# Expert up products taken in fp32 as they lie, instead of in three products of fp32r halves

## What is computed

```python
def moe_ff(x, gate_w, w1, w2, w3):
    scores = xf @ gate_w
    topk_scores, topk_idx = jax.lax.top_k(scores, TOPK)
    topk_probs = jax.nn.softmax(topk_scores, axis=-1)
    weight = jnp.sum(jax.nn.one_hot(topk_idx, EXPERTS, dtype=xf.dtype) * topk_probs[..., None], axis=1)
    h = jax.nn.silu(jnp.einsum('td,edh->eth', xf, w1)) * jnp.einsum('td,edh->eth', xf, w2)
    out_e = jnp.einsum('eth,ehd->etd', h, w3)
    out = jnp.einsum('etd,te->td', out_e, weight)
```

## Time and profile before

| | |
|---|---|
| time, median of 3 runs | 2132.61 us (2127.89 to 2138.53) |
| the profiled execution | 2133.48 us, its span on the core 2131.9 us |
| granted TensorE clock, mean | 0.852 |
| TensorE busy over the span | 1599.4 us (75%) in 19079 matmul instructions |
| VectorE busy | 1275.6 us (60%) |
| ScalarE busy | 1043.0 us (49%) |
| GpSimd busy | 347.0 us (16%) |
| up products (L1410) | 384 matmul instructions into `e_ps_a`, 384 into `e_ps_b` |
| down products (L1425) | 256 matmul instructions |

### The profile page before, as it was taken

One profiled execution on the slowest core, in us unless ns is written; L12 is line 12 of the kernel. 1 busy time (PEld: TensorE's weight loads), 2 busy tenths in 40 slices (PEclk: granted clock), 3 DMA queues, 4 the chain that ended last, 5 costly groups with the idle time before them and its releaser, 6 DMA issues. The chain is left out here.

```text
span 2131.9 us, 53638 instructions
## 1 busy us (share of the span) xinstructions
PE 1599.4 (75%) x19079; PEld 991.3 (46%) x19079; DVE 1275.6 (60%) x3054; ACT 1043.0 (49%) x1996; POOL 347.0 (16%) x677
## 2 busy tenths in 40 slices
PE   6544477777539999975349988798889788989647
PEld 3222244444326666643125555455555455556423
DVE  6932776676256766743206666565667565667636
ACT  4422166566323233214236666565667466667233
POOL 4433254454320000002200000000000000000023
PEclk8866599899659999987658999898989798889869
DMA  2157222222451211217898999898999899999521
GB/s 69 45 167 225 58 64 55 55 64 47 117 179 45 94 70 54 102 36 210 244 294 294 345 354 345 306 359 292 370 337 360 302 337 352 343 350 331 175 66 59
DMA packets 189941, 424.95 MB, mean 199 GB/s; under 512 B 37296, under 2 KB 85328, under 8 KB 180272
## 3 DMA queue, kind: packets, MB, share of 16 engines
q1 hardware_dynamic: 165856, 241.52, 36.9%
q10 hardware_dynamic: 13104, 150.80, 17.3%
q0 software_dynamic: 10720, 29.11, 5.3%
HBM read 218.07 MB, written 203.03 MB: 198 GB/s over the span
## 5 line engine op out<-in xcount | busy, mean ns | idle before, releaser
L2133 DVE CUSTOM_DVE_ANT_0 r_shifted<-r_ps_ac,r_shifted 128x512 f32<-128x512 f32 x512 | 352.1, 688 | 336.0 <-PE r_ps_ac L2010 319.4
L2099 ACT ACTIVATE r_probs<-r_ps_keys 128x512 f32<-128x512 f32 x512 | 309.5, 605 | 296.8 <-PE r_ps_keys L2017 262.3
L2078 ACT ACTIVATE r_wide<-r_ps_wide 128x512 f32<-128x512 f32 (+1 forms) x576 | 329.2, 590 | 72.2 <-PE r_ps_wide L2001 71.0
L2017 PE MATMUL r_ps_keys<-r_ident,r_shifted 128*128 128x128 f32 x2048 | 337.2, 291 | 3.4 <-issue 1.4
L2017 PEld LDWEIGHTS r_ps_keys<-r_ident,r_shifted 128*128 128x128 f32 x2048 | 277.0, 151 | 62.9 <-issue 20.2
L2001 PE MATMUL r_ps_wide<-r_r,r_qv 48*32 48x64 bf16 (+12 forms) x6144 | 240.9, 259 | 50.8 <-issue 34.1
L2010 PE MATMUL r_ps_ac<-r_k,r_qu 128*128 128x512 bf16 x512 | 214.1, 419 | 68.6 <-DMA r_v<-v 31.7
L2141 DVE TENSOR_SCALAR r_shifted<-r_shifted,r_mx 128x512 f32<-128x512 f32 x512 | 249.2, 487 | 18.3
L915 ACT ACTIVATE c_probs<-c_ps_keys 128x512 f32<-128x512 f32 (+1 forms) x384 | 174.8, 531 | 152.2 <-PE c_ps_keys L841 152.0
L2001 PEld LDWEIGHTS r_ps_wide<-r_r,r_qv 48*32 48x32 bf16 x6144 | 103.8, 96 | 151.4 <-issue 150.0
L2028 PE MATMUL r_ps_out<-r_probs,r_v 128*9 128x128 f32 x4096 | 155.7, 290 | 23.7 <-issue 23.0
(11 more groups left out here) (215 smaller groups left out, 2106.2 us busy)
## 6 DMA issues: line engine op xcount, KB each, us to landing
skew<-r_wide ACTq DMA_DIRECT2D x64, 2224.0 KB, 11.8
r_shifted<-skew SPq DMA_DIRECT2D x64, 2048.0 KB, 17.2
e_weight_all<-weights SPq DMA_DIRECT2D x8, 2048.0 KB, 7.5
c_qk<-qk_stacks POOLq DMA_DIRECT2D x64, 192.0 KB, 3.7
stack<-d_part SPq DMA_DIRECT2D x96, 128.0 KB, 2.6
qk_stacks<-b_part SPq DMA_DIRECT2D x48, 128.0 KB, 3.4
qk_stacks<-b_part POOLq DMA_DIRECT2D x48, 128.0 KB, 3.7
stack<-d_part POOLq DMA_DIRECT2D x48, 128.0 KB, 3.8
```

The costliest lines, as they stand in the source:

```text
L2017: last = pe.transpose(ps_keys[u % 2][:, j * P:(j + 1) * P], shifted[:, s, u, j * P:(j + 1) * P], ident[:, :])
L2078: act.activation(wide[:, s, c, lo:hi], ps_wide[bk % BANKS][:, 0:hi - lo], ACT.Copy).then_inc(wide_sb, 1)
L2099: act.activation(probs[:, h % 2, :, b * P:(b + 1) * P], ps_keys[u % 2][:, :].rearrange("p (j i) -> p j i", j=NT), ACT.Exp, scale=SCALE).th ...
L2133: dve.tensor_tensor_reduce(out=shifted[:, s, u, :], in0=ps_ac[u % 2][:, :], in1=shifted[:, s, u, :], scale=1.0, scalar=LOWEST, op0=ALU.add ...
```

## The change

w1, w2 and `hT` are handed to TensorE as they are, in fp32. The half tiles, the casts and subtractions on DVE and POOL, and their semaphores go. `up` issues one matmul for each k instead of three. In the loop, TensorE waits for `hT` itself (`hT_sb`) ahead of the first product of a new block. At the start, the up products of expert 0 wait for their own weights alone and are issued ahead of `turn_weights(0)`, where they stood behind it.

```diff
             def up(w, ps, e, s, ready):
                 for k in range(KH):
-                    for i, (a, b) in enumerate(HALVES):
-                        last = pe.matmul(ps[:, k, :], w[a][:, e, k * P:(k + 1) * P], hT_halves[b][:, s, :],
-                                         start=(i == 0), stop=(i == 2))
+                    last = pe.matmul(ps[:, k, :], w[:, e, k * P:(k + 1) * P], hT[:, s, :], start=True, stop=True)
                 last.then_inc(ready, 1)
...
                         if e + 2 == NE:
-                            pe.wait_ge(hT_low, n + 2)
+                            pe.wait_ge(hT_sb, n + 2)
                         ups(n + 1, 1 - s, e + 2 - NE)
...
             pe.wait_ge(consts, n_const)
             route(0, 0, 16)
+            pe.wait_ge(w_loaded[0], 16)
+            up(w1, ps_a, 0, 0, a_ps)
+            pe.wait_ge(w_loaded[1], 16)
+            up(w2, ps_b, 0, 0, b_ps)
             turn_weights(0)
-            pe.wait_ge(hT_low, 1)
-            pe.wait_ge(w_low, 1)
-            up(w1_halves, ps_a, 0, 0, a_ps)
-            pe.wait_ge(w_low, 2)
-            up(w2_halves, ps_b, 0, 0, b_ps)
             ups(0, 0, 1)
             pe.wait_ge(w_loaded[2], 16)
             steps(step, pe)
...
                     if e == 0 and ahead:
                         best(n + 1)
-                        high_tokens(n + 1, 1 - s)
...
             best(0)
-            high_tokens(0, 0)
             weights(0)
             take_rows(0)
-            for i, (w, halves) in enumerate(((w1, w1_halves), (w2, w2_halves))):
-                dve.wait_ge(w_loaded[i], 16)
-                high(halves[0][:, :, :], w[:, :, :], w_high)
-                dve.wait_ge(w_high, i + 1)
-                dve.tensor_tensor(halves[1][:, :, :], w[:, :, :], halves[0][:, :, :],
-                                  ALU.subtract).then_inc(w_low, 1)
             for e in range(2):
                 product(e, e, 0, 1)
```

More of the change, by code:

```diff
@@ L1221, in phase_experts @@
         w3 = sb("w3", [P, NE, HID])
-        w1_halves = [sb(f"w1_half{i}", [P, NE, HID], F32R) for i in range(2)]
-        w2_halves = [sb(f"w2_half{i}", [P, NE, HID], F32R) for i in range(2)]
         gate = sb("gate", [P, NE])
@@ L1230, in phase_experts @@
         hT = sb("hT", [P, 2, L])
-        hT_halves = [sb(f"hT_half{i}", [P, 2, L], F32R) for i in range(2)]
         scores = sb("scores", [P, NT, NE])
@@ L1278, in phase_experts @@
         gu_sb = sem("gu_sb")
[L1279 to L1282, removed]
         w_loaded = [sem(f"w{i}_loaded") for i in (1, 2, 3)]
@@ L1359, in _ @@
         def _(pool):
[L1360 to L1363, removed]
             def step(it, s, first, ahead):
@@ L1367, in step @@
                 for e in range(NE):
-                    if e == 0 and ahead:
-                        low_tokens(n + 1, 1 - s)
                     if e == 3 and not first:
@@ L1373, in _ @@
             norm.constants(pool)
-            low_tokens(0, 0)
             steps(step, pool)
@@ L1379, in _ @@
         def _(pe):
-            HALVES = ((0, 0), (0, 1), (1, 0))
             def route(n, s, load_count):
@@ L1416, in ups @@
                 pe.wait_ge(silu_sb, m + 1)
-                up(w1_halves, ps_a, e, s, a_ps)
+                up(w1, ps_a, e, s, a_ps)
                 pe.wait_ge(gu_sb, m + 1)
-                up(w2_halves, ps_b, e, s, b_ps)
+                up(w2, ps_b, e, s, b_ps)
             def down(m, s, e):
@@ L1537, in take_rows @@
                 dve.tensor_copy(weight_rows[:, :], ps_s[0:NE, 0:L]).then_inc(rows_sb, 1)
[L1539 to L1544, removed]
             def product(m, e, s, loads):
```

## The result

| | before | changed |
|---|---|---|
| time, median | 2130.25 us (2122.72 to 2138.53, 4 runs) | 2155.26 us (2149.89 to 2166.61, 4 runs) |
| ratio | | 1.0142, 95% interval 1.0101 to 1.0183 |
| the profiled execution | 2133.48 us, span 2131.9 | 2153.25 us, span 2151.8 |

Two further sets of runs of the changed kernel gave 1.0109 (1.0068 to 1.0150) and 1.0116 (1.0075 to 1.0157). So the direction was right and the size too large by some 15 us (+40.4 forecast). Ratios are of fast executions alone: the profile of e3 is of a slow one (1201.10 us), and of e10's six executions one of 6671.60 us is left out of its ratio.

A forecast was written before the change was run, and what follows sets the result against it. It took TensorE's instruction issue to bound the experts' loop. 2133.5 us profiled + 38.7 (loop) + 1.7 (start) = 2173.9; that execution being 0.9 above the median, the forecast was 2173.0 us, range 2165 to 2182.

The forecast's parts named there:

- The loop: Experts' loop: each of 61 rounds grows from 4.51 to 5.15 us on TensorE, +38.7 us (36.6 to 40.9).
- Passes against rows: Up products: passes alone give 0.93 us more a round; the trace's durations give 0.635, which the forecast took.
- The start: Experts' start: first product 9.7 us earlier, but the spread load lands later; first down product +1.7 us (-1.6 to +5).
- (1): Rival: the start keeps its 9.7 us because the spread load lands in time; 2161.6 us, chance 0.03.
- (2): Rival: passes alone count, so the loop's up products grow by a third, 56.9 us; 2191 us, chance 0.03.
- (3): Rival: each fp32 up instruction streams like a half product, 0.233 us, gaining 0.93 a round; 2077 us, chance 0.02.
- (4): Rival: the clock doesn't hold 1.00 in the loop with more fp32; about 2215 us, chance 0.04.
- The later phases shifted alone: Phases behind the experts: they would start later but keep their lengths, so they add nothing to the sum.

The follow-up runs named there:

- e3: The kernel before without the phase of relative attention, the merge reading the first attention's sums instead: 1185.92 us.
- e10: The changed kernel with 160 semaphore increments on TensorE at the start of the relative attention: 2189.47 us, ratio 1.0274.
- e4: The changed kernel without the phase of relative attention, the merge reading the first attention's sums instead: 1228.34 us.
- e16: The kernel before with TensorE semaphore increments: 40 at the experts' start, 40 at their end, 80 at the relative attention's start: 2116.69 us, ratio 0.9937.
- e13: The kernel before with 80 semaphore increments at the end of TensorE's experts and 80 at the relative attention's start: 2122.31 us, ratio 0.9974.
- e14: The changed kernel with 80 semaphore increments at the end of TensorE's experts and 80 at the relative attention's start: 2182.30 us, ratio 1.0238.

## Why the prediction was wrong

- **The loop, +38.7 us: right.** e3 and e4 give 301.2 and 339.9 us from the first down product to the last, 38.7. The first profile of the changed kernel has 342.6; there the granted clock was 0.50 until 660 us, 4.5 us behind the first down product, which the forecast had at the start's upper end.
- **Passes against rows: the row held.** The Trainium skill (FP8 and Floating Point Precision, TensorE Precision Notes) counts four passes for fp32. By passes the loop would have grown by 57 us; it grew by 38.7. The up products of a round went from 2.80 to 3.43 us, a factor of 1.23 and not 4/3. By that page's count the 0.858 us of an fp32 product would be four passes of 0.215 us each, against three of 0.233, which gives the 1.23; how a product is split into passes no row shows.
- **The start, +1.7 us (-1.6 to +5): right in mechanism, and in size within its bounds.** The landing of the spread weights took over as the last wait, TensorE idled 6.4 us (some 6 forecast) and the first down product came 36.9, 34.6 and 34.9 us after the phase's first load against 34.4, 33.5 and 34.2, so +2.5, +1.1 and +0.7. Of some 10 us by which the first product was early nothing was left. The rivals are out: (1) the gain wasn't kept, (2) passes don't count alone, (3) each up product of an expert is four fp32 instructions at 0.43 us, and (4) the granted clock was 1.00 from 670 to 990 us.
- **"The later phases shifted alone": this step failed.** It was a term of the sum, the change in the phases behind the experts, set to zero without a row. Measured, the relative attention alone became 23 to 37 us shorter. The change takes 385 instructions out of TensorE's code ahead of a loop that fetches its code anew at each turn, and the loop of the relative attention came to need 15 packets a turn instead of 16. The term is about -23 us by the table above (-14 by the medians of e16). 2173 - 23 = 2150, against 2155 measured. None of my rivals held it. The trace of the kernel before could have raised the question: the steps with the loop's turn took 38.2 us on the mean and the others some 26, and TensorE stood there with no releaser but "issue". Its timeline at the first turn:

```profile
1345.71 0.60 PE L2010 MATMUL r_ps_ac<-r_k,r_qu 128*128 128x512 bf16 x1 [5.77 <-issue]
```

It could not have given the sign, which hangs on where the code ends up.
- What is left, 3 to 6 us between 42.4 - 22.9 = 19.5 and the 22.6 to 25.0 measured, is within the scatter of the phases ahead of the experts and not explained. The chances named for a slower kernel add up to 0.98 and not 0.97, which changes nothing.
- Open is how the place makes the wait. Each turn has one packet more and its step is 4 to 5 us longer, but the wait at the jump is as long with 15 packets as with 16; that it is the extra packet that is waited for, at another point of the step, is argued, not shown. With 16 packets a turn the phase took 939 to 953 us at three places of the loop, so the count may not be all of it.

## What to carry to other kernels

Here an fp32 product and one of three fp32r halves differed by less than their passes; take both distances from the weight loads of the trace. A first product made earlier is worth what is queued behind it: here it pushed back a transpose of 0.6 us on which a 2 MB load hung, and putting the transpose first gained 4.4 us by the profiles (5.9 by the medians). In this program a large loop whose DMA engines are nearly always busy moved the whole time by about a per cent with the place of its code, so an edit of the code ahead can do this; compare phases and not whole times, and try a few places of the code before an edit of that size is judged.

## What the runs showed of the hardware

- TensorE's code arrives in packets of 16 KB (2.75 MB in 168 packets in the kernel before), and a loop of 3486 instructions is fetched again at every turn: 15 or 16 packets, according to where it begins (114 or 115 packets in the phase, or 118 to 120). While the DMA engines are 93 to 97% busy the step with the turn takes 7 to 15 us more than the other steps, in the first two profiles of each kernel.
- 80 semaphore increments in a row on TensorE ahead of a long wait in the relative attention didn't delay its first wide product (14.7 us after the phase's first load in e13 and e14, as before; 16.0 in e16), and cost 4.7 us where they ran into a barrier; 160 at one place delayed that product by 12 us.
- A matmul of 512 columns on fp32r operands has a distance of 0.233 us at clock 1.00, and one on fp32 operands is two instructions 0.43 us apart.
